# Softmax rows turned into columns by four 32x32 block transposes of VectorE, in place of one TensorE transpose

## The reference, cut to what matters

```python
# layer 0, mask = nodemask
q, k = split(X @ Wqk, 2);  v = X @ Wv
agg = einsum('bij,bjd->bid', adj, k * mask[:, :, None])
w   = inv_scale * mask * einsum('bid,bid->bi', q, agg)
L   = softmax(w, axis=1)[:, :, None] * v          # one weight per node, softmax over the 128 nodes
x   = layernorm(x + L)
# layer 1
weight = adj * exp(query @ key^T);  weight /= sum(weight, axis=2)
x   = layernorm(x + weight @ value)
```

## Time and profile before

| | |
|---|---|
| median of 3 runs | 296.91 us (296.63 to 296.96) |
| the profiled execution | 296.95 us, its span 295.2 us (1.75 us lie outside the span) |
| mean granted TensorE clock | 0.994 of full speed |
| PE / PEld busy | 287.0 us (97%) / 266.6 us (90%) |
| DVE / ACT / POOL busy | 235.1 (80%) / 224.7 (76%) / 220.3 us (75%) |

### The profile page before, as it was taken

How to read it: one execution, slowest core, us unless ns; L and a number is a source line. 1 busy time by engine, 2 the same in 40 slices (tenths; PEclk the granted TensorE clock), 3 DMA queues, 4 the chain that set the end, 5 groups by cost and what they waited for, 6 DMA issues and landing times.

```text
span 295.2 us, 7074 instructions
## 1 busy us (share of the span) xinstructions
PE 287.0 (97%) x2012; PEld 266.6 (90%) x2012; DVE 235.1 (80%) x728; ACT 224.7 (76%) x539; POOL 220.3 (75%) x269
## 2 busy tenths in 40 slices
PE   7999999999999999999999999999999999999991
PEld 7789999999999999999999999999999999999980
DVE  1478888888878888888888888788887888888784
ACT  3455768788788878878887887878788787887763
POOL 1556988877888877788887778978777897877331
PEclk9999999999999999999999999999999999999997
DMA  6921234322344432324443232444323243210102
GB/s 231 338 91 37 89 92 126 93 95 85 109 124 125 125 96 86 95 96 125 125 125 92 86 101 94 125 125 125 93 85 92 103 125 125 89 55 25 50 36 107
DMA packets 19165, 31.26 MB, mean 106 GB/s; under 512 B 2128, under 2 KB 6608, under 8 KB 19152
## 3 DMA queue, kind: packets, MB, share of 16 engines
q1 hardware_dynamic: 19152, 31.11, 34.2%
HBM read 22.71 MB, written 8.39 MB: 105 GB/s over the span
## 4 chain that ended last, share of the span: by engine, by line
PE 94%; DMA 2%; issue 1%; DVE 1%; ACT 0%; POOL 0%; SPq 0%; POOLq 0%; DVEq 0%
PE ps L866 25%; PE ps L868 24%; PE ps L867 24%; PE ps L967 9%; PE ps L949 5%; DMA p<-params 2%; PE ps L917 1%; PE ps L923 1%; PE ps L889 1%; PE ps L1101 1%; PE ps L972 1%; DVE x L649 0%; PE ps L928 0%; PE ps L936 0%; POOLq L36 0%
## 5 line engine op out<-in xcount | busy, mean ns | idle before, releaser
L866 PE MATMUL ps<-w_hi,xt_hi 128*128 128x512 f32 x124 | 49.9, 402 | 0.0
L868 PE MATMUL ps<-w_hi,xt_lo 128*128 128x512 f32 x124 | 48.8, 393 | 0.0
L867 PE MATMUL ps<-w_lo,xt_hi 128*128 128x512 f32 x124 | 48.5, 391 | 0.0
L452 ACT ACTIVATE x<-x_sum,shift,rstd 128x256 f32<-128x256 f32 x60 | 32.9, 595 | 17.0 <-POOL shift L377 17.0
L363 POOL TENSOR_TENSOR edge_lo<-edge,edge_hi 128x256 fp32r<-128x256 f32 x29 | 21.5, 740 | 29.5 <-ACT edge_hi L532 29.5
L296 POOL TENSOR_TENSOR x1b<-x,bv_all 128x512 f32<-128x512 f32 x31 | 40.2, 1297 | 2.6 <-DVE x L805 1.7
L350 POOL TENSOR_TENSOR xt_lo<-xt_raw,xt_hi 128x512 fp32r<-128x512 f32 x31 | 40.1, 1294 | 1.8 <-ACT xt_hi L434 1.8
L467 ACT ACTIVATE z<-ps,z_bias 128x256 f32<-128x256 f32 x62 | 26.0, 472 | 19.7 <-PE ps L868 19.7
L374 POOL TENSOR_TENSOR rstd<-var_eps,minus_half 128x4 f32<-128x4 f32 x31 | 33.2, 1071 | 9.3 <-DVE var_eps L783 9.3
L866 PE MATMUL ps<-wv_hi,x1t_hi 128*128 128x258 f32 x124 | 37.8, 305 | 0.0
L357 POOL TENSOR_TENSOR x_lo<-x_raw,x_hi 128x512 fp32r<-128x512 f32 x28 | 36.2, 1293 | 0.0
(11 more groups left out here) (162 smaller groups left out, 880.3 us busy)
## 6 DMA issues: line engine op xcount, KB each, us to landing
xt_raw<-xt_pairs SPq DMA_DIRECT2D x32, 256.0 KB, 2.7
x_raw<-x_pairs SPq DMA_DIRECT2D x32, 256.0 KB, 2.7
out_pairs<-x SPq DMA_DIRECT2D x31, 256.0 KB, 2.0
adjt<-adjt_pairs SPq DMA_DIRECT2D x32, 129.0 KB, 2.1
p<-params SPq DMA_DIRECT2D x1, 770.0 KB, 6.7
p<-params SPq DMA_DIRECT2D x1, 512.0 KB, 3.8
p<-params SPq DMA_DIRECT2D x1, 256.0 KB, 4.7
out_pairs<-x SPq DMA_DIRECT2D x2, 128.0 KB, 1.8
```

The lines of the kernel that those rows point to most:

```text
L452: last = nc.scalar.activation(out[:, graph(g)], in_[:, graph(g)], ACT.Identity, bias=shift[r % 2][:, layer, g:g + 1], scale=rstd[r % 2][:, ...
L866: nc.tensor.matmul(out, s_hi, m_hi, start=first, stop=False)
L867: nc.tensor.matmul(out, s_hi, m_lo, start=False, stop=False)
L868: return nc.tensor.matmul(out, s_lo, m_hi, start=False, stop=last)
```

## The change

The scaled rows are no longer written to SBUF but to rows 0 and 1 of PSUM bank 6, columns 128 to 255. DVE then waits for its own write and does four block transposes of 32 rows by 32 columns, each out of PSUM to one group of 32 partitions of `p_col`, which is now 128x32 (columns 0 and 1 are the weights, the others are transposes of whatever stands in rows 2 to 31). The last one raises `p_col_done`. BLOCK is 32. PE's `transpose_p` is gone from all its places, as is the copy to `p_col` and the wait for it. The tile p_row stays under the name `warm` for the warm-up matmuls. The wait for the identity matrix moves to `transpose_w`.

```diff
-        p_row = sb("p_row", [128, 128])
-        p_col = sb("p_col", [128, 2])
+        warm = sb("warm", [128, 128])
+        p_col = sb("p_col", [128, BLOCK])
...
-        def p_full_ps(r):
-            return yv_ps(r)[:, 1, 0:NODES]
-
-        def p_col_ps(r):
-            return p_full_ps(r)[:, 0:2]
+        def p_row_ps(r):
+            return yv_ps(r)[0:BLOCK, 1, NODES:2 * NODES]
...
             def sum_x1(u, r):
                 dve.wait_ge(p_col_done, u + 1)
-                nc.vector.tensor_copy(p_col[:, :], p_col_ps(r)).then_inc(p_copied, 1)
                 if exists(u - 2):
                     dve.wait_ge(x1_done, u - 1)
-                dve.wait_ge(p_copied, u + 1)
...
                     dve.wait_ge(inv_sum_done, t + 3)
-                    if exists(t + 1):
-                        dve.wait_ge(p_col_done, t + 2)
-                    nc.vector.tensor_scalar(p_row[0:2, :], exp_row_ps(r + 2), inv_sum[:, 0:1], None, ALU.mult)\
+                    nc.vector.tensor_scalar(p_row_ps(r + 2)[0:2, :], exp_row_ps(r + 2), inv_sum[:, 0:1], None, ALU.mult)\
                         .then_inc(p_row_done, 1)
+                    dve.wait_ge(p_row_done, t + 3)
+                    for b in range(0, NODES, BLOCK):
+                        block = nc.vector.transpose(p_col[b:b + BLOCK, :], p_row_ps(r + 2)[:, b:b + BLOCK])
+                    block.then_inc(p_col_done, 1)
...
-            def transpose_p(u, r):
-
-                pe.wait_ge(ident_ready, 1)
-                pe.wait_ge(p_row_done, u + 1)
-                nc.tensor.transpose(p_full_ps(r), p_row[:, :], ident[:, :]).then_inc(p_col_done, 1)
...
                 if r != DRAIN:
-                    transpose_p(t + 2, r + 2)
                     transpose_next(t, r)
```

More of the change, by code:

```diff
@@ L26 @@
 SPLIT = 4
+BLOCK = 32
 def exists(pair):
@@ L142, in build @@
         ident_zeroed, ident_ready, consts_ready = sem("ident_zeroed"), sem("ident_ready"), sem("consts_ready")
-        p_row_zeroed = sem("p_row_zeroed")
+        warm_zeroed = sem("warm_zeroed")
         bqk_done, bqk_summed, ones_ready = sem("bqk_done"), sem("bqk_summed"), sem("ones_ready")
@@ L163, in build @@
         x1_sum_done, w_done = sems("x1_sum_done", 2), sems("w_done", 2)
-        row_max_done, inv_sum_done, p_row_done, p_copied = sem("row_max_done"), sem("inv_sum_done"), sem("p_row_done"), sem("p_copied")
+        row_max_done, inv_sum_done, p_row_done = sem("row_max_done"), sem("inv_sum_done"), sem("p_row_done")
         stats1_done, x1t_hi_done, x1t_lo_done = sem("stats1_done"), sem("x1t_hi_done"), sem("x1t_lo_done")
@@ L403, in slot @@
                     add_value_bias(r + 1)
-            nc.gpsimd.memset(p_row[:, :], 0.0).then_inc(p_row_zeroed, 1)
+            nc.gpsimd.memset(warm[:, :], 0.0).then_inc(warm_zeroed, 1)
             nc.gpsimd.memset(ident[:, :], 0.0).then_inc(ident_zeroed, 1)
@@ L908, in project @@
                     mm = project_half(u, r, g, k)
-                    if r == 2 and g == 0 and k == 0:
-                        transpose_p(1, 1)
                 mm.then_inc(yv_done[g], 1)
             def transpose_w(u, r):
+                pe.wait_ge(ident_ready, 1)
                 for g in range(2):
@@ L1070, in slot @@
                     values(x1t_hi, x1t_lo, 1).then_inc(val_done, 1)
-                    if r == DRAIN:
-                        transpose_p(t + 2, r + 2)
                     pe.wait_ge(z_copied, t + 1)
@@ L1081, in slot @@
                 if r != DRAIN:
-                    transpose_p(t + 2, r + 2)
                     transpose_next(t, r)
-            pe.wait_ge(p_row_zeroed, 1)
+            pe.wait_ge(warm_zeroed, 1)
             for _ in range(WARM_UP):
-                nc.tensor.matmul(ps[:, 0, 0:128], p_row[:, :], p_row[:, :], start=True, stop=True)
+                nc.tensor.matmul(ps[:, 0, 0:128], warm[:, :], warm[:, :], start=True, stop=True)
             pe.wait_ge(wqk_loaded, 16)
@@ L1115, in _ @@
             aggregate(1, 1)
-            transpose_p(0, 0)
             project(1, 1, 0)
```

## The result

The changed kernel takes 297.39 us, the median of 20 runs (296.77 to 297.91), against 296.92 us for the kernel before (20 runs, 296.22 to 297.06): a ratio of 1.0017, 95% interval 1.0011 to 1.0024. It is slower by about 0.5 us, less than the 0.2% that I had called no change, but clear of its interval and to the other side than forecast. 297.39 lies in the range of 292.8 to 299.3; the 295.8 forecast was 1.6 us too low, and a gain of 1.2 us was forecast where 0.5 was lost.

What follows compares the result with a forecast made beforehand. It took PE's own instructions and DVE's chain from softmax row to sum, nearly level, as the bound. Slots -2.0, end +0.6 and start +0.2 gave -1.2 us on 296.95: 295.8 us, range 292.8 to 299.3.

Steps and rivals of the forecast that it cites:

- The two paths that end close together: Per slot, PE's own instructions and DVE's chain from softmax row to sum end within some hundredths of a us.
- The blocks one after the other: DVE's four block transposes run in sequence without a full hand-over: 0.215 us each, 0.86 for four.
- The end: In slot DRAIN the blocks delay x1t_lo_a and pair 31's sum, with PE idle there: +0.6 us.
- What is pushed: bias_scores starts at 139.02, not 138.55; ACT's exponential waits for it; the edges move by no more than 0.05 us.
- the last link of DVE's part: DVE's row to sum: hand-over 0.04, blocks 0.86, bias_scores to the sum 0.10; 1.00 us against 1.07 before.
- the 2.0 us: Gain in the steady slots: the sum and PE's load 0.07 us earlier in each of 28 slots.
- the five edges of the loop: Loop-edge slots counted like the others; DVE's branch, delaying the sum there by 0.1 us, stays.
- The start: Pair 0's sum +0.28 us, PE saves about 0.1 on transposes: +0.2 us.
- The rival nearest to what happened: No gain: bias_scores' delay passes on, or PE's transpose hid something; only ends count, 296.95 to 297.7 us; chance 0.07.
- the slower rival: A block costs 0.25 us, DVE's chain passes 1.07, PE's projection 0.07 later per slot: 300.1 us; chance 0.20.
- its own range: The main forecast's range, 294.2 to 297.2 us, for 0.20 to 0.23 us a block; chance 0.45.
- The overlapping rival: DVE's blocks overlap, 0.09 to 0.19 us each, PE bound by its own instructions: 292.8 us, 293.7 at 0.19; chance 0.28.

Runs made afterwards that it cites:

- the fifth blocks: Changed kernel plus an unread fifth block, written to the fourth's partition group (300.12 us, ratio 1.0119) or to another group (305.35 us, ratio 1.0301).
- all blocks to one group: Changed kernel with all four blocks written to partitions 0 to 31 at different columns of a wider p_col: 293.93 us, ratio 0.9907.
- one block: Changed kernel with only the first of the four blocks done, leaving out the weights of 96 nodes: 292.79 us, ratio 0.9872.
- row in SBUF: Changed kernel with the scaled row written to SBUF and read there by the four blocks: 295.83 us, ratio 0.9972.
- order reversed: Changed kernel with the four blocks in the order 3, 2, 1, 0, the last to partitions 0 to 31: 294.16 us, ratio 0.9921.
- pairs 0, 1, 2 and 31 by PE: Changed kernel with these pairs back on PE's transpose and copy, the others by blocks in order 0 to 3: 295.92 us, ratio 0.9972.
- the two together: Changed kernel with pairs 0, 1, 2 and 31 by PE's old way and the other pairs' blocks in order 3, 2, 1, 0: 293.06 us, ratio 0.9875.

## Why the prediction was wrong

**Right.** The two paths that end close together, with `x1_sum_done[0]` as the releaser: shown by the fifth blocks. The blocks one after the other at 0.215 us: measured 0.22, four in 0.87 where 0.86 stood. By the Trainium skill ("VectorE: DVE Perf Modes", section "Two Vector instructions with no wait between them") an instruction whose output starts in another quadrant of 32 partitions than the last one into that memory is held until all earlier ones have finished. That is borne out here: 0.22 us between starts with the output's group of partitions changing, 0.10 to 0.14 without, and bias_scores 0.10 us earlier against the last block's end when its group is that block's. The end: +0.6 forecast, +0.6 measured, by way of x1t_lo_a and the sum (PE's queries of pair 30 come 0.53 us later behind slot 28's scores, its transposes of pair 31 0.63 later; 0.58 and 0.64 were forecast). What is pushed: the exponential waits for bias_scores (139.89 to 140.20) and the edges keep their place behind the sum.

**The step that failed** is the last link of DVE's part: bias_scores to the sum, for which I took 0.10 us. It measured 0.17: 0.03 from the last block's end to bias_scores, which is held like the blocks, and 0.14 from there to the sum. I had named bias_scores as held but given its hand-over no time, and I took the spacing after it from a pair of other small operations and a semaphore wait. The kernels with all blocks to one group, with one block and with a fifth block have the same 0.14; which property of the two operations makes it 0.14 and not 0.06 is open. The sum 0.04 + 0.86 + 0.10 = 1.00 became 0.03 + 0.87 + 0.17 = 1.07, the same as before the change, and the 0.07 us that each of the slots was to gain is nothing. Of the 2.0 us, 0.2 are left in the usual slots.

The other 0.6 us of the slots' gain come from a place where I had counted wrongly to the other side: the five edges of the loop. I had DVE's branch delay the sum there by 0.1 us as before. It did not. How long after the slot's first load of the scores DVE starts the sum, in the usual slot shown above and in the one at an edge, two slots later:

| us | usual slot | at the edge |
|---|---|---|
| before: the copy, then the sum | 1.32, 1.58 | 1.42, 1.68 |
| changed | 1.55 | 1.55 |
| row in SBUF | 1.52 | 1.52 |
| order reversed | 1.41 | 1.49 |
| one block | 1.08 | 1.49 |

At an edge the sum starts at 1.49 at the earliest, however early it is due; one that is due later loses nothing. In the changed kernel it is due at 1.55, behind the longer chain, and that is why the edges cost nothing there. In the kernel before, the copy was due ahead of the branch's end and took the sum with it. Where the reversed order or one block makes the sum early, the edges cost again: these slots are 0.03 to 0.10 us longer than the others of their kernel.

**The start** is the second term of a wrong size: +0.2 forecast, +0.6 measured. I had traced pair 0 only, and there the row to the sum went from 0.72 to 0.94 us, less than the 0.28 more that I had put. Pair 2 I had not looked at: in slot 0 PE's way took 0.74 us from the row to the sum and the blocks take 1.07, the projection has no slack for it, and PE waited 0.57 us. The kernel with pairs 0, 1, 2 and 31 by PE has start and end back in full.

With the slots, the end and the start as measured the sum is -0.8 + 0.6 + 0.6 = +0.4 us, and the medians have +0.5. The rival nearest to what happened is the one that I gave 0.07: no gain in the slots, only the ends count, 296.95 to 297.7. Its place was another one (I had put it in the edges' path), so as a mechanism it was wrong; the measured one is the slower rival's, VectorE's chain, stopped at its point of balance. I had given the chain's room as 0.07 us and called the block's length the unknown that decides, and did not spend the same care on the short links around it, which together have the same size. That the edges gave back 0.6 us, and so kept the loss at 0.5, was luck.

Two figures of the prediction do not follow from its own terms. The upper end of its own range, 0.23 us a block, is -0.3 + 0.65 + 0.25 on 296.95, about 297.6 and not 297.2, so that 297.39 lies inside it. The overlapping rival at 0.19 a block is 296.95 - 3.9 - 0.4 + 0.6, about 293.2 and not 293.7.

## What to carry to other kernels

When two engines' paths end within a tenth of a microsecond, taking work off one gives only as much as the other's path gets shorter too; write down every hand-over of the new chain, the small operation behind the added ones too, since each counts once per slot. The block transposes of VectorE that wrote to changing groups of 32 partitions were charged their whole duration here; put last the one whose group the next instruction writes. A rewrite that pays in the steady slots may cost in the first and the last ones, where nothing covers it: there the old way can stay, and the two together gave 3.7 us, 1.25%.

## What the runs showed of the hardware

A 32x32 fp32 block transpose of VectorE took 0.206 us out of PSUM and 0.202 out of SBUF when it was held by the one before, and 0.161 when it overlapped it, at 0.10 to 0.14 us between starts. The order of four such blocks, with nothing else changed, moved the kernel's ratio from 1.0017 to 0.9921. The transpose of a 128x128 block on TensorE took 0.11 us of its stream of loads, and its removal, together with the wait for VectorE, 0.11 us off the usual slot; its matmul's duration is 0.27.
